# Token front of a language model tower on one Trainium2 core: first normalization and projections by halves, loads in another order

## The chip, the core and the metric

The kernel runs on one NeuronCore of a Trainium2 chip. Its engines work side by side, each through a list of instructions of its own in order, and wait for each other by semaphores: TensorE (PE, matmuls, with its weight loads shown as PEld), VectorE (DVE), ScalarE (ACT), GpSimd (POOL) and SyncE (SP, which here only issues DMAs). Matmul results stand in PSUM (`ps`, eight banks of 512 columns), all else in SBUF with 128 partitions. The metric is the device time of one execution in microseconds, the median of several runs.

## The reference, cut to what matters

Two sequences of 1024 tokens, 64 channels. The change touches the first two lines and the network `_rpe` inside the third block.

```python
h = W[x] + pe                                             # embedding + position table
h = h + linear_attn(layernorm(h), Wq, Wkv, Wproj, bproj)  # block 1
h = h + ffn(layernorm(h), ...)      # block 2: causal attention with rotary tables, 8 experts, top 2
h = h + tno(layernorm(h), ...)      # block 3: Toeplitz mixing by FFT, gate, branch
h = h + layernorm(h) @ weight.T + bias

# block 1, eight heads of eight channels
q = elu(q) + 1; k = elu(k) + 1
context = k^T v ; out = (q context) / max(q . sum(k), 1e-6) @ Wproj.T + bproj

# in block 3: the lag network, 3 layers over the lags alone, no token in it
h = idx @ pos_w.T + pos_b
for i in range(3): h = relu(srms(h)) @ rpe_lw[i].T + rpe_lb[i]
a = relu(srms(h)) @ out_w.T + out_b
```

`srms` divides by the root of the mean square over 8 channels. The kernel computes elu(x) + 1 as max(x, 0) + exp(min(x, 0)).

## The kernel before

The tokens stand in eight tiles of 128 tokens, each with both sequences' 64 channels side by side. Half 0 is tiles 0 to 3 and half 1 tiles 4 to 7, 512 columns each. The order on every engine is written out by hand: `build` has one block per engine, which it runs from top to bottom.

- **SP** (L341 to L413) issues the loads in this order: indices, `rp` (lag network), `idt` (identity), `pe_s` (positions, on `ld_pe`), the whole weight pack `w` (on `ld_w`), the rotary tables `rope_s` and `rope_k`, `bfc_s` (bf16 constants, among them the warmers' operands), two small ones. Then it waits for all gathers and issues the Fourier table `tm` and the expert weights.
- **POOL** (L416) issues sixteen gathers of embedding rows (L428), one for each tile and sequence, counted in three semaphores by `SLICES = ((0, 4), (4, 6), (6, 8))`. Later it adds the bias to `h` (L440), once both halves are normalized, and clears `va2`.
- **DVE** (L1507) runs the lag network first: `rpe_layer(0..2)` and its end `rpe_layer(3)` (L1592 to L1613), which holds the reciprocal of L1611. Then `embed(a)` for the three slices (L1615: add positions, row sums, subtract the mean), `first_sums(a)` (row sums of the squares), one variance for all (L1641), one reciprocal, and `scale_rows` for both halves (L1644, line L1567 in the profile). Then `xT` of half 1 is copied from PSUM, the transposed lag network is folded into `geo` (L1647 to L1655), and the features follow in pairs: k minima, key sums, q minima, query sums (L1659 to L1680). `cbd` is the block context, masked (L1683, L1684).
- **ACT** (L1197) takes the square roots of the lag network (L1242), the squares of the slices (`first_squares`, L1234), one root (L1247), the copy of `xT` for half 0, loads the table for Exp, and does the exponentials and the copies of v (`va1`). `next_function` (L1224) is a table load with a dummy operation.
- **PE** (L629) runs the lag network's matmuls, its two transposes (L665, L666), `keep_warm(14, 6)` (fourteen matmuls whose result nobody reads), `transposes` of both halves (L636), then k for both halves, v for both, q for both (L673 to L682), the context (L684) and the products with `cbd` (L692). `mm` is the helper at L336, whose line nearly all matmuls show.

A float32 matmul of this kernel shows as two instructions in the trace, each with a weight load of its own.

## Time and profile before

| | |
|---|---|
| median of 3 runs | 327.52 us (327.43 to 327.71) |
| profiled execution, its time | 327.58 us |
| its span (first to last instruction) | 325.8 us |
| PE busy | 291.7 us (90%) |
| DVE busy | 232.7 us (71%) |
| ACT busy | 148.2 us (45%) |
| POOL busy | 118.6 us (36%) |
| mean granted TensorE clock | 0.991 |

The busy shares are means over a long program. The change is in the first 40 us, so the tables that count are the timelines of that stretch, which show for each engine when an instruction or a run of like instructions began, how long it took, and for whom the engine had waited. A time in them is counted from the span's start.

### The profile page before, as it was taken

Reading aid. Unit: us, or ns where it says so; the run is one execution under the profiler, and the core shown is the slowest. Engines: PE = TensorE matmul, PEld = TensorE weight load, DVE = VectorE, ACT = ScalarE, POOL = GpSimd, SP = SyncE. Lnnn points to the kernel's source line nnn. Section 1 sums busy time; section 2 is a strip of 40 time slices with the busy share of each in tenths; the row PEclk is TensorE's granted clock in tenths of the full one; section 3 lists DMA queues with packets and bytes.
Section 4 is the critical chain, followed back from the end, with each engine's and each line's share of the span. In section 5 each row is a group of like instructions: output and inputs, shape, how many; then the busy total and the mean of one; then the engine's idle time right before and its main releaser. Section 6 shows DMA issues by size and latency. Waiting matters only on the chain.

```text
span 325.8 us, 4437 instructions
## 1 busy us (share of the span) xinstructions
PE 291.7 (90%) x1564; PEld 165.8 (51%) x1575; DVE 232.7 (71%) x428; ACT 148.2 (45%) x249; POOL 118.6 (36%) x168
## 2 busy tenths in 40 slices
PE   1548989999999999999999999999999999999863
PEld 1214754753332434576654555554655555557552
DVE  1577888889989778568955686744678576675576
ACT  2113634752576777846638454544533110022283
POOL 5773000331428244303323460431004689920212
PEclk9999999999999999999999999999999999999996
DMA  7957500285000000600000000000000000000001
GB/s 237 347 114 292 231 0 0 36 152 106 2 3 2 2 3 4 257 0 2 1 0 2 1 0 2 0 0 2 1 0 0 2 0 0 3 0 0 0 3 64
DMA packets 6270, 15.24 MB, mean 47 GB/s; under 512 B 1384, under 2 KB 3816, under 8 KB 5608
## 3 DMA queue, kind: packets, MB, share of 16 engines
q1 hardware_dynamic: 5685, 14.41, 14.5%
q0 software_dynamic: 512, 0.53, 0.7%
q8 instruction: 13, 0.21, 0.3%
q14 instruction: 9, 0.07, 0.1%
q10 hardware_dynamic: 51, 0.01, 0.0%
HBM read 12.01 MB, written 0.52 MB: 38 GB/s over the span
## 4 chain that ended last, share of the span: by engine, by line
PE 63%; DVE 16%; POOL 8%; issue 5%; ACT 5%; DMA 1%; another core or an unknown queue 0%; DVEq 0%; ACTq 0%
PE ps L336 60%; POOL xc L428 5%; DVE rw L1766 2%; DVE arena L1900 1%; PE ps L842 1%; DVE h L2027 1%; DMA xc<-emb,idx_s 1%; POOL share L605 1%; PE ps L636 1%; ACT L1224 1%; PE ps L1117 1%; DVE xs L1827 1%; POOL share L606 1%; ACT arena L1403 1%; DMA idx_s<-idx 0%
## 5 line engine op out<-in xcount | busy, mean ns | idle before, releaser
L1766 DVE TENSOR_REDUCE rw<-ps 128x1 f32<-128x512 f32 (+2 forms) x80 | 45.8, 629 | 7.1 <-PE ps L336 6.8
L1343 ACT ACTIVATE arena<-ps 128x1024 f32<-128x1024 f32 (+3 forms) x48 | 37.5, 812 | 21.8 <-PE ps L336 21.4
L336 PE MATMUL ps<-arena 96*128 96x512 bf16 (+7 forms) x192 | 43.2, 327 | 0.4 <-DVE rw L1766 0.2
L336 PE MATMUL ps<-xs,e_hi 128*128 128x512 f32 x96 | 40.5, 422 | 1.5 <-ACT arena L1403 0.8
L1403 ACT ACTIVATE arena<-ps 128x512 f32<-128x512 f32 x48 | 28.5, 597 | 28.1 <-PE ps L336 23.8
L1900 DVE TENSOR_TENSOR arena<-ps,arena 128x512 f32<-128x512 f32 x48 | 32.5, 687 | 11.3 <-ACT arena L1403 9.8
L336 PE MATMUL ps<-xs,e_lo 128*128 128x512 f32 x96 | 37.9, 395 | 0.0
L336 PE MATMUL ps<-bfc_s 128*128 128x512 bf16 (+2 forms) x108 | 28.4, 334 | 1.7 <-DVE xc L1623 1.5
L336 PEld LDWEIGHTS ps<-arena 96*128 96x128 bf16 (+1 forms) x192 | 15.9, 97 | 25.6 <-DVE rw L1766 11.8
L336 PE MATMUL ps<-arena,ew 64*64 64x512 f32 (+1 forms) x128 | 24.2, 609 | 1.7 <-issue 1.4
L336 PEld LDWEIGHTS ps<-xs,e_hi 128*128 128x128 f32 x96 | 18.0, 188 | 14.4 <-issue 7.2
L510 POOL TENSOR_SCALAR_AFFINE_SELECT arena<-arena 128x256 f32<-128x256 f32 (+1 forms) x32 | 15.1, 475 | 28.1 <-ACT arena L1343 27.7
L336 PE MATMUL ps<-arena,tables 128*128 128x384 f32 x64 | 21.9, 488 | 0.3 <-DVE share L2040 0.3
L336 PE MATMUL ps<-share,tables 128*128 128x384 f32 x64 | 21.8, 489 | 0.0
L336 PE MATMUL ps<-arena,va 128*32 128x512 f32 (+3 forms) x192 | 21.6, 506 | 0.2 <-POOL arena L510 0.2
L1581 DVE TENSOR_TENSOR arena<-ps,arena 128x512 f32<-128x512 f32 x16 | 10.4, 687 | 14.9 <-PE ps L336 7.5
L336 PE MATMUL ps<-w,xT 128*128 128x128 f32 (+2 forms) x144 | 19.7, 321 | 1.4 <-ACT xT L1387 1.1
L336 PEld LDWEIGHTS ps<-xs,e_lo 128*128 128x128 f32 x96 | 18.1, 189 | 2.6
L336 PEld LDWEIGHTS ps<-w,xT 128*128 128x128 f32 (+1 forms) x144 | 14.3, 188 | 9.1 <-issue 6.1
L428 POOL DMA_INDIRECT xc<-emb,idx_s x16 | 16.3, 1020 | 6.7 <-issue 4.6
L1394 ACT ACTIVATE arena<-ps 128x384 f32<-128x384 f32 x16 | 7.8, 490 | 23.4 <-PE ps L336 23.4
L1224 ACT ACT_TABLE_LOAD x14 | 18.0, 1283 | 1.0 <-PEq L2292 0.8
(273 smaller groups left out, 511.3 us busy)
## 6 DMA issues: line engine op xcount, KB each, us to landing
arena<-arena SPq DMA_DIRECT2D x24, 96.0 KB, 2.8
w<-wpack SPq DMA_DIRECT2D x1, 2089.5 KB, 10.8
arena<-tm SPq DMA_DIRECT2D x2, 1024.0 KB, 5.8
tables<-epack SPq DMA_DIRECT2D x1, 1540.0 KB, 11.0
arena<-rope SPq DMA_DIRECT2D x1, 1024.0 KB, 13.4
tables<-tu SPq DMA_DIRECT2D x2, 512.0 KB, 3.7
tables<-tk SPq DMA_DIRECT2D x2, 512.0 KB, 5.6
rp<-rpack SPq DMA_DIRECT2D x1, 678.5 KB, 4.1
```

The lines of the kernel that those rows point to most:

```text
L336: return nc.tensor.matmul(o, l, r, start=start, stop=stop, **kw)
L428: nc.gpsimd.indirect_dma_start(xc[:, j, b, :], None, emb, bass.IndirectOffsetOnAxis(ap=idx_s[:, n:n + 1], axis=0)).then_inc(gathered[[lo < ...
L510: nc.gpsimd.affine_select(out=v, in_=v, pattern=[[0, 2], [1, P + behind]], compare_op=ALU.is_ge, fill=0.0, base=-behind, channel_multiplie ...
L605: nc.gpsimd.tensor_tensor(dst[:, 0], p1[:, 0], p1[:, 1], ALU.subtract).then_inc(S("part"), 1)
L606: nc.gpsimd.tensor_tensor(dst[:, 1], p2[:, 0], p2[:, 1], ALU.add).then_inc(S("part"), 1)
L1224: nc.scalar.activation(unused[:, loads[0]:loads[0] + 1], idt[0:1, 0:1], func)
L1343: nc.scalar.activation(pt[:, n % PT_SLOTS, :, lo:512], ps[:, bank:bank + 2, lo:512], ACT.Exp, scale=HD ** -0.5).then_inc(S("exp_done"), 1)
L1394: nc.scalar.activation(dst.rearrange("p (b c) -> p b c", b=B), ps[:, UV_BANKS[k]:UV_BANKS[k] + 2, 0:D1], ACT.Silu).then_inc(S("uv_silu"), 1)
L1403: nc.scalar.activation(sil[:, m % 2], ps[:, m % 2], ACT.Silu).then_inc(S("silu"), 1)
L1581: V.tensor_tensor(zp_[:, n % 2], ps[:, 5 + n % 2], wb[:, n % 2], ALU.mult).then_inc(S("zpair"), 1)
L1766: V.tensor_reduce(top_view(m, part)[:, at:at + len(heads), i], src, AXX, ALU.max, negate=True).then_inc(S("ring_read"), 1)
L1900: V.tensor_tensor(gh[:, n % GSLOTS, n3], ps[:, 2 + m % 3], sil[:, m % 2], ALU.mult).then_inc(S("gated"), 1)
```

## The change

**Loads.** The columns of the weight pack are put in another order, so that what block 1 needs (`q1`, `kv1`, `proj1`, `bproj`, the masks) stands first, 784 of 4179 columns. This part is loaded alone, on `ld_pe` with the positions; `bfc` comes next, then the rest of `w`. The rotary tables are issued only once slice 0 is gathered.

**Order by halves.** The lag network's end is no longer one piece: its square stands behind `embed(0)`, and its root, reciprocal and last product behind the scale of half 0. Each half has a root and a scale of its own (`first_root`, `first_scale`, with the epsilon now as ACT's bias). PE projects half 0 (`first_projections(0)`: T1, k, v, q) ahead of the lag network's transposes and ten warmers, and half 1 behind them. ACT takes over both `xT` copies and the k and q minima of half 0, as Relu(-x), with exp(-x) of the result later. On DVE the first key sum stands ahead of the k minimum of half 1. POOL's bias add waits for `geo_done` as well.

```diff
-for _n, _w in (("q1", P), ("kv1", 2 * P), ("proj1", P), ("q2", P), ("q2r", P), ("k2", 64), ("k2r", 64), ("v2", 64),
+for _n, _w in (("q1", P), ("kv1", 2 * P), ("proj1", P), ("bproj", P), ("mask_c", P), ("mask_k", 16),
+               ("q2", P), ("q2r", P), ("k2", 64), ("k2r", 64), ("v2", 64),
                ("wo2", P), ("v3", 2 * D1), ("u3", 2 * D1), ("o3", 3 * P), ("t3", P), ("w4", P),
-               ("bproj", P), ("ub", 2 * D1), ("vb", 2 * D1), ("ob", 1), ("tb", P), ("b4", P), ("ln2", 1),
-               ("ln1", 1), ("cen", P), ("mask_c", P), ("mask_k", 16), ("eidx", P), ("enum", P)):
+               ("ub", 2 * D1), ("vb", 2 * D1), ("ob", 1), ("tb", P), ("b4", P), ("ln2", 1),
+               ("ln1", 1), ("cen", P), ("eidx", P), ("enum", P)):
     WCOLS[_n] = (_at, _at + _w)
     _at += _w
 WTOT = _at
+WFRONT = WCOLS["mask_k"][1]
...
-            sp.dma_start(w[:], wpack).then_inc(ld_w, 16)
-            sp.dma_start(rope_s[:], rope).then_inc(ld_rope, 16)
-            for c in range(2):
-                sp.dma_start(rope_k[64 * c:64 * c + 64], rope[0:64, :, c * 512:(c + 1) * 512]).then_inc(ld_rope, 16)
+            sp.dma_start(w[:, 0:WFRONT], wpack[:, 0:WFRONT]).then_inc(ld_pe, 16)
             sp.dma_start(bfc_s[:], bfc).then_inc(ld_bf, 16)
+            sp.dma_start(w[:, WFRONT:WTOT], wpack[:, WFRONT:WTOT]).then_inc(ld_w, 16)
             at = 3 * P + B * NPAIR * P
             for b in range(B):
                 sp.dma_start(kst[MROW:KROWS, b * NKV:b * NKV + NKV].rearrange("p g t -> p (g t)").rearrange("p (n t) -> p n t", t=P),
                              spread(bfc[0:65:32, at:at + P], 1, NKV * N // P)).then_inc(ld_ones, 16)
             for a, (lo, hi) in enumerate(SLICES):
                 sp.wait_ge(gathered[a], 16 * B * (hi - lo))
+                if a == 0:
+                    sp.dma_start(rope_s[:], rope).then_inc(ld_rope, 16)
+                    for c in range(2):
+                        sp.dma_start(rope_k[64 * c:64 * c + 64], rope[0:64, :, c * 512:(c + 1) * 512]).then_inc(ld_rope, 16)
...
             pool.wait_ge(S("n1"), 2)
-            pool.wait_ge(ld_w, 16)
+            pool.wait_ge(S("geo_done"), 2 * NW)
+            pool.wait_ge(ld_pe, 32)
...
+            def first_projections(a):
+
+                pe.wait_ge(S("n1"), a + 1)
+                for j in range(4 * a, 4 * a + 4):
+                    ins = nc.tensor.transpose(ps[:, 2 + a, j % 4 * P:(j % 4 + 1) * P], sq[:, j].rearrange("p b c -> p (b c)"), idt[:])
+                ins.then_inc(S("T1"), 1)
+                pe.wait_ge(ld_pe, 32)
+                pe.wait_ge(S(("xT1_lo", "xT1_hi")[a]), 1)
+                for x in range(2):
+                    for j in range(4 * a, 4 * a + 4):
+                        ins = mm(ps[:, 2 * x + a, j % 4 * P:(j % 4 + 1) * P], xT[:, j * P:(j + 1) * P], W("kv1", x * P, (x + 1) * P))
+                    ins.then_inc(S("kv1"), 1)
+                mm(ps[:, 4 + a], W("q1"), xT[:, a * 512:(a + 1) * 512]).then_inc(S("q1"), 1)
+
+            first_projections(0)
             pe.wait_ge(S("r_act"), LAYERS + 1)
             nc.tensor.transpose(ps[:, 7, 0:P], rh[:, 3, 0:P], idt[:])
             nc.tensor.transpose(ps[:, 7, P:2 * P], rh[:, 3, P:2 * P], idt[:]).then_inc(S("r_T"), 1)
             pe.wait_ge(ld_bf, 16)
-            pe.wait_ge(S("first_centred"), 1)
-            keep_warm(14, 6)
-
-            transposes(sq, 2, S("n1"), S("T1"))
-            pe.wait_ge(ld_w, 16)
-            for x in range(2):
-                for j in range(NT):
-                    if x == 0 and j % 4 == 0:
-                        pe.wait_ge(S(("xT1_lo", "xT1_hi")[j // 4]), 1)
-                    ins = mm(ps[:, 2 * x + j // 4, (j % 4) * P:(j % 4 + 1) * P], xT[:, j * P:(j + 1) * P],
-                             W("kv1", x * P, (x + 1) * P))
-                    if j % 4 == 3:
-                        ins.then_inc(S("kv1"), 1)
-            for c in range(2):
-                mm(ps[:, 4 + c], W("q1"), xT[:, c * 512:(c + 1) * 512]).then_inc(S("q1"), 1)
+            pe.wait_ge(S("first_centred"), 3)
+            keep_warm(10, 6)
+            first_projections(1)
...
+            def first_root(a):
+
+                act.wait_ge(S("mean_squares"), NORMS["var1"] + a)
+                nc.scalar.activation(st[:, 3, 8 * a:8 * a + 8], st[:, 1, 8 * a:8 * a + 8], ACT.Sqrt, scale=1.0 / C,
+                                     bias=eps1[:]).then_inc(S("roots"), 1)
+
+            def first_columns(a):
+
+                act.wait_ge(S("T1"), a + 1)
+                nc.scalar.copy(xT[:, 512 * a:512 * a + 512], ps[:, 2 + a]).then_inc(S(("xT1_lo", "xT1_hi")[a]), 1)
+
+            def first_values(a):
+
+                act.wait_ge(S("kv1"), 2 * a + 2)
+                nc.scalar.copy(va1[:, 4 * a:4 * a + 4, 0:P], ps[:, 2 + a].rearrange("p (j x) -> p j x", j=4)).then_inc(S("va1"), 1)
+
+            for i in range(LAYERS):
+                lag_root(i)
+            first_squares(0)
+            lag_root(LAYERS)
+            act.wait_ge(S("geo_constants"), 1)
+            first_root(0)
+            first_columns(0)
+            first_squares(1)
+            act.wait_ge(S("kv1"), 1)
+            nc.scalar.activation(kf1[:, 0:4].rearrange("p j b c -> p (j b c)"), ps[:, 0], ACT.Relu, scale=-1.0).then_inc(S("kmin"), 1)
+            first_values(0)
+            act.wait_ge(S("q1"), 1)
+            nc.scalar.activation(qf1[:, 0:512], ps[:, 4], ACT.Relu, scale=-1.0).then_inc(S("qmin"), 1)
+            first_squares(2)
+            first_root(1)
             next_function(ACT.Exp)
-            for a in range(2):
-                act.wait_ge(S("kmin"), a + 1)
-                nc.scalar.activation(kf1[:, 4 * a:4 * a + 4], kf1[:, 4 * a:4 * a + 4], ACT.Exp).then_inc(S("kexp"), 1)
-            for a in range(2):
-                act.wait_ge(S("kv1"), a + 3)
-                nc.scalar.copy(va1[:, 4 * a:4 * a + 4, 0:P], ps[:, 2 + a].rearrange("p (j x) -> p j x", j=4)).then_inc(S("va1"), 1)
-            for c in range(2):
-                act.wait_ge(S("qmin"), c + 1)
-                nc.scalar.activation(qf1[:, c * 512:(c + 1) * 512], tmp[:, c * 512:(c + 1) * 512], ACT.Exp).then_inc(S("qexp"), 1)
+            first_columns(1)
+            act.wait_ge(S("kmin"), 1)
+            nc.scalar.activation(kf1[:, 0:4], kf1[:, 0:4], ACT.Exp, scale=-1.0).then_inc(S("kexp"), 1)
+            act.wait_ge(S("qmin"), 1)
+            nc.scalar.activation(qf1[:, 0:512], qf1[:, 0:512], ACT.Exp, scale=-1.0).then_inc(S("qexp"), 1)
+            act.wait_ge(S("kmin"), 2)
+            nc.scalar.activation(kf1[:, 4:8], kf1[:, 4:8], ACT.Exp).then_inc(S("kexp"), 1)
+            first_values(1)
+            act.wait_ge(S("qmin"), 2)
+            nc.scalar.activation(qf1[:, 512:N], tmp[:, 512:N], ACT.Exp).then_inc(S("qexp"), 1)
...
+            def first_scale(a):
+
+                dve.wait_ge(S("roots"), NORMS["std1"] + a)
+                step(V.reciprocal(hst(4, a), hst(3, a)))
+                V.tensor_tensor(half3(sq, a), half3(xc, a), spread(hst(4, a), 2, C), ALU.mult).then_inc(S("n1"), 1)
+
+            def first_total(a):
+
+                lo, hi = SLICES[a]
+                dve.wait_ge(S("first_squared"), a + 1)
+                V.tensor_reduce(st[:, 1, B * lo:B * hi], sq[:, lo:hi].rearrange("p j b c -> p (j b) c"), AXX,
+                                ALU.add).then_inc(S("mean_squares"), 1)
+
+            for i in range(LAYERS):
                 rpe_layer(i)
-            dve.wait_ge(ld_pe, 16)
+            dve.wait_ge(ld_pe, 32)
             embed(0)
+            V.tensor_tensor(rh[:, 1], rh[:, 0], rh[:, 0], ALU.mult).then_inc(S("r_sq"), 1)
+            first_total(0)
+            first_scale(0)
+            dve.wait_ge(S("r_rms"), LAYERS + 1)
+            V.scalar_tensor_tensor(out=scale_r, in0=scale_r, scalar=1e-8, in1=rh[:, 2], op0=ALU.mult, op1=ALU.add).then_inc(S("r_scale"), 1)
+            dve.wait_ge(S("r_scale"), LAYERS + 1)
+            step(V.reciprocal(scale_r, scale_r))
+            V.scalar_tensor_tensor(out=rh[:, 3], in0=rh[:, 0], scalar=0.0, in1=scale_r, op0=ALU.max, op1=ALU.mult).then_inc(S("r_act"), 1)
             embed(1)
-            first_sums(0)
+            first_sums(1)
             embed(2)
-            first_sums(1)
-            first_sums(2)
-            V.tensor_scalar(st[:, 2], st[:, 1], 1.0 / C, 1e-5, ALU.mult, ALU.add).then_inc(S("mean_squares"), 1)
-            dve.wait_ge(S("roots"), NORMS["std1"])
-            step(V.reciprocal(st[:, 4], st[:, 3]))
-            scale_rows(sq, xc, 4, S("n1"))
-            evac(3, S("T1"), 2, S("xT1_hi"))
             dve.wait_ge(S("r_T"), 1)
             step(V.tensor_copy(rh[:, 1], ps[:, 7, 0:2 * P]))
+            first_total(2)
+            first_scale(1)
             others = rh[:, 1, 64:NW * 64].rearrange("p (d x) -> p d x", d=NW - 1)
             step(V.tensor_tensor(others, others, spread(rh[:, 1, 0:64], 1, NW - 1), ALU.subtract))
             dve.wait_ge(S("geo_constants"), 2)
@@ -1653,22 +1710,22 @@
                                for sd in range(2))
                 V.tensor_tensor(geo[:, 0, :, d * GR:d * GR + R], plus, minus, ALU.add).then_inc(S("geo_done"), 1)
                 V.tensor_tensor(geo[:, 1, :, d * GR:d * GR + R], plus, minus, ALU.subtract).then_inc(S("geo_done"), 1)
-            dve.wait_ge(S("xT1_lo"), 1)
-            dve.wait_ge(S("xT1_hi"), 1)
 
             k2 = kf1.rearrange("p j b c -> p (j b c)")
-            for a in range(2):
-                g = slice(512 * a, 512 * a + 512)
-                dve.wait_ge(S("kv1"), a + 1)
-                V.tensor_scalar(k2[:, g], ps[:, a], 0.0, None, ALU.min).then_inc(S("kmin"), 1)
-            for a in range(2):
+
+            def key_features(a):
+
                 g = slice(512 * a, 512 * a + 512)
                 dve.wait_ge(S("kexp"), a + 1)
                 V.scalar_tensor_tensor(out=k2[:, g], in0=ps[:, a], scalar=0.0, in1=k2[:, g], op0=ALU.max,
                                        op1=ALU.add).then_inc(S("kf1"), 1)
-            for c in range(2):
-                dve.wait_ge(S("q1"), c + 1)
-                V.tensor_scalar(tmp[:, c * 512:(c + 1) * 512], ps[:, 4 + c], 0.0, None, ALU.min).then_inc(S("qmin"), 1)
+
+            key_features(0)
+            dve.wait_ge(S("kv1"), 3)
+            V.tensor_scalar(k2[:, 512:N], ps[:, 1], 0.0, None, ALU.min).then_inc(S("kmin"), 1)
+            dve.wait_ge(S("q1"), 2)
+            V.tensor_scalar(tmp[:, 512:N], ps[:, 5], 0.0, None, ALU.min).then_inc(S("qmin"), 1)
+            key_features(1)
```

On DVE, from the last full lag layer to the first slice's square sums and on to the second slice, there stood:

```order
L1608 SCALAR_TENSOR_TENSOR share<-tmp,rp,ps 128x256 [waits r_lin,r_scale]
L1596 TENSOR_TENSOR share<-share 128x256 [waits dve_chain]
L1603 SCALAR_TENSOR_TENSOR tmp<-tmp,share 128x256 [waits r_rms]
L1611 RECIPROCAL tmp<-tmp 128x256 [waits r_scale]
L1612 SCALAR_TENSOR_TENSOR share<-share,tmp 128x256 [waits dve_chain]
L1621 TENSOR_TENSOR h<-xc,share 128x512 [waits gathered_0,ld_pe]
L1622 TENSOR_REDUCE st<-h 128x8 [waits dve_chain]
L1623 SCALAR_TENSOR_TENSOR xc<-st,h 128x512 [waits dve_chain]
L1621 TENSOR_TENSOR h<-xc,share 128x256 [waits gathered_1]
L1622 TENSOR_REDUCE st<-h 128x4 [waits dve_chain]
L1623 SCALAR_TENSOR_TENSOR xc<-st,h 128x256 [waits dve_chain]
L1630 TENSOR_REDUCE st<-sq 128x8 [waits first_squared]
```

and there stands (L1694 to L1697 are the lag network's end, L1676 and L1677 the scale of half 0):

```order
L1649 SCALAR_TENSOR_TENSOR share<-tmp,rp,ps 128x256 [waits r_lin,r_scale]
L1662 TENSOR_TENSOR h<-xc,share 128x512 [waits gathered_0,ld_pe,dve_chain]
L1663 TENSOR_REDUCE st<-h 128x8 [waits dve_chain]
L1664 SCALAR_TENSOR_TENSOR xc<-st,h 128x512 [waits dve_chain]
L1690 TENSOR_TENSOR share<-share 128x256
L1683 TENSOR_REDUCE st<-sq 128x8 [waits first_squared]
L1676 RECIPROCAL st<-st 128x8 [waits roots]
L1677 TENSOR_TENSOR sq<-xc,st 128x512 [waits dve_chain]
L1694 SCALAR_TENSOR_TENSOR tmp<-tmp,share 128x256 [waits r_rms]
L1696 RECIPROCAL tmp<-tmp 128x256 [waits r_scale]
L1697 SCALAR_TENSOR_TENSOR share<-share,tmp 128x256 [waits dve_chain]
L1662 TENSOR_TENSOR h<-xc,share 128x256 [waits gathered_1]
```

The embedding, the sums and the scale of half 0 have moved ahead of the reciprocal of the lag network; the second slice comes behind it.

On ACT, from the lag network's last roots to the table load for Exp, there stood:

```order
L1242 ACTIVATE share<-ps 128x256 [waits r_ss]
L1242 ACTIVATE share<-ps 128x256 [waits r_scale,r_ss] x3
L1234 ACTIVATE sq<-xc 128x512 [waits first_centred]
L1234 ACTIVATE sq<-xc 128x256 [waits first_centred] x2
L1247 ACTIVATE st<-st 128x16 [waits mean_squares]
L1210 COPY xT<-ps 128x512 [waits T1]
L1224 ACT_TABLE_LOAD
L1224 ACTIVATE unused<-idt 1x1
```

and there stands (L1254 is the lag root, L1281 the k minimum of half 0, L1284 its q minimum, L1245 the squares):

```order
L1245 ACTIVATE sq<-xc 128x512 [waits first_centred]
L1254 ACTIVATE share<-ps 128x256 [waits r_scale,r_ss]
L1259 ACTIVATE st<-st,eps 128x8 [waits mean_squares,geo_constants]
L1265 COPY xT<-ps 128x512 [waits T1]
L1245 ACTIVATE sq<-xc 128x256 [waits first_centred]
L1281 ACTIVATE share<-ps 128x512 [waits kv1]
L1270 COPY share<-ps 128x4x128 [waits kv1]
L1284 ACTIVATE share<-ps 128x512 [waits q1]
L1245 ACTIVATE sq<-xc 128x256 [waits first_centred]
L1259 ACTIVATE st<-st,eps 128x8 [waits mean_squares]
L1235 ACT_TABLE_LOAD
```

The squares of the third slice now stand behind three instructions that read half 0's projections from PSUM.

On PE, behind the lag network's last matmul, there stood:

```order
L336 MATMUL ps<-share,rp 128x256 [waits r_sq]
L665 MATMUL ps<-idt,share 128x128 [waits r_act]
L666 MATMUL ps<-idt,share 128x128
L336 MATMUL ps<-bfc_s 128x512 [waits first_centred,ld_bf]
L336 MATMUL ps<-bfc_s 128x512 x13
L636 MATMUL ps<-idt,sq 128x128 [waits n1]
L636 MATMUL ps<-idt,sq 128x128 x3
L636 MATMUL ps<-idt,sq 128x128 [waits n1]
L636 MATMUL ps<-idt,sq 128x128 x3
L336 MATMUL ps<-w,xT 128x128 [waits xT1_lo,ld_w]
L336 MATMUL ps<-w,xT 128x128 x3
```

and there stands (L675 are the transposes of a half, L687 and L688 those of the lag network):

```order
L339 MATMUL ps<-share,rp 128x256 [waits r_sq]
L675 MATMUL ps<-idt,sq 128x128 [waits n1]
L675 MATMUL ps<-idt,sq 128x128 x3
L339 MATMUL ps<-w,xT 128x128 [waits xT1_lo,ld_pe]
L339 MATMUL ps<-w,xT 128x128 x7
L339 MATMUL ps<-xT,w 128x512
L687 MATMUL ps<-idt,share 128x128 [waits r_act]
L688 MATMUL ps<-idt,share 128x128
L339 MATMUL ps<-bfc_s 128x512 [waits first_centred,ld_bf]
L339 MATMUL ps<-bfc_s 128x512 x9
L675 MATMUL ps<-idt,sq 128x128 [waits n1]
```

The transposes, the eight k and v matmuls and the q matmul of half 0 have moved ahead of the lag network's transposes and the warmers.

## Rows read from the trace of the kernel before

**Rows 1.** The page, chain that ended last: shares of the span by engine
```profile
PE 63%; DVE 16%; POOL 8%; issue 5%; ACT 5%; DMA 1%; another core or an unknown queue 0%; DVEq 0%; ACTq 0%
```

**Rows 2.** Timeline, DVE and ACT: start us, us, engine, line, operation, [idle before]
```profile
15.35 0.48 DVE L1608 SCALAR_TENSOR_TENSOR share<-tmp,rp,ps 128x256 f32<-128x256 f32 x1
...
18.48 1.75 DVE L1611 RECIPROCAL tmp<-tmp 128x256 f32<-128x256 f32 x1
...
20.61 0.68 DVE L1621 TENSOR_TENSOR h<-xc,share 128x512 f32<-128x512 f32 x1
...
22.78 0.63 ACT L1234 ACTIVATE sq<-xc 128x512 f32<-128x512 f32 x1 [4.79 <-DVE xc L1623]
...
25.25 0.43 DVE L1621 TENSOR_TENSOR h<-xc,share 128x256 f32<-128x256 f32 x1 [0.66 <-DMA xc<-emb,idx_s]
...
26.63 0.42 ACT L1234 ACTIVATE sq<-xc 128x256 f32<-128x256 f32 x1 [2.18 <-DVE xc L1623]
...
27.81 0.22 ACT L1247 ACTIVATE st<-st 128x16 f32<-128x16 f32 x1 [0.76 <-DVE st L1641]
28.06 0.25 DVE L1643 RECIPROCAL st<-st 128x16 f32<-128x16 f32 x1 [0.28 <-ACT st L1247]
28.34 1.29 DVE L1567 TENSOR_TENSOR sq<-xc,st 128x512 f32<-128x512 f32 x2
```

**Rows 3.** Landing of the eighth gather, of the last two gathers, and of `w`
```profile
DMA to landing us min/median/max: 7.5/7.5/7.5
...
DMA to landing us min/median/max: 2.7/2.8/2.8
...
w<-wpack SPq DMA_DIRECT2D x1, 2089.5 KB, 10.8
```

**Rows 4.** Timeline, PE and PEld: last lag matmuls, the warmers, their last weight loads
```profile
16.35 1.22 PE L336 MATMUL ps<-share,rp 128*128 128x256 f32 x2 [1.10 <-DVE share L1596]
...
22.89 4.83 PE L336 MATMUL ps<-bfc_s 128*128 128x512 bf16 x14 [1.45 <-DVE xc L1623]
...
26.26 0.97 PEld L336 LDWEIGHTS ps<-bfc_s 128*128 128x128 bf16 x5 [0.28 <-issue]
```

**Rows 5.** Timeline of PE at the kernel's end; busy time by stretch (clock: last but two)
```profile
312.87 1.06 PE L336 MATMUL ps<-w4c,xT 128*128 128x128 f32 x8
...
319.72 2.02 PE L336 MATMUL ps<-w4c,xT 128*128 128x128 f32 x8 [0.79 <-ACT xT L1483]
...
320.00:321.00 1.00, 1.00 (x6) 1.00 (x6) 0.97 (x3) 0.60 (x1) 0.14 (x1) 0.50 0.00 0
```

**Rows 6.** Timeline, all engines, from the transposes to the products with `cbd`
```profile
29.72 2.36 POOL L440 TENSOR_TENSOR h<-h,w 128x1024 f32<-128x1024 f32 x1 [5.19 <-DVE sq L1567]
29.79 0.59 ACT L1210 COPY xT<-ps 128x512 f32<-128x512 f32 x1 [1.76 <-PE ps L636]
...
30.39 1.28 ACT L1224 ACT_TABLE_LOAD   x1
...
30.52 3.81 PE L336 MATMUL ps<-w,xT 128*128 128x128 f32 x32 [0.17 <-ACT xT L1210]
...
31.44 0.79 DVE L1649 TENSOR_TENSOR share<-share 128x128 f32<-128x128 f32 x1
...
34.16 1.88 PE L336 MATMUL ps<-xT,w 128*128 128x512 f32 x4
...
36.85 1.31 DVE L1677 SCALAR_TENSOR_TENSOR share<-ps,share 128x512 f32<-128x512 f32 x2
...
38.08 0.28 DVE L1683 TENSOR_TENSOR cbd<-ps,w 128x128 f32<-128x128 f32 x1
...
38.56 2.23 PE L336 MATMUL ps<-cbd,share 128*128 128x144 f32 x16 [0.73 <-DVE cbd L1684]
```

**Rows 7.** Timeline, DVE and POOL side by side in the expert stage
```profile
150.16 0.68 DVE L1900 TENSOR_TENSOR arena<-ps,arena 128x512 f32<-128x512 f32 x1
...
150.32 0.32 POOL L547 TENSOR_TENSOR rw<-rw 128x64 f32<-128x64 f32 x1 [1.11 <-DVE rw L1861]
```

More of the change, by code:

```diff
@@ L45 @@
                                              "wpc_zero"))}
-NORMS = {"var1": 1, "var2": 2, "var2b": 4, "var3": 5, "var3b": 6, "var4": 7,
-         "std1": 1, "std2": 2, "rms2b": 4, "std3": 5, "rms3b": 6, "std4": 7}
+NORMS = {"var1": 1, "var2": 3, "var2b": 5, "var3": 5, "var3b": 6, "var4": 7,
+         "std1": 1, "std2": 3, "rms2b": 5, "std3": 5, "rms3b": 6, "std4": 7}
 EARLY_AF = 3
@@ L297, in build @@
         unused = sb("unused", [1, 16])
+        eps1 = sb("eps1", [P, 1])
         w4c = sb("w4c", [P, P])
@@ L566, in _ @@
             candidates(1, 1)
-            pool.wait_ge(S("mean_squares"), 5)
+            pool.wait_ge(S("mean_squares"), 6)
             PT(st[:, 3, 0:8], st[:, 2, 0:8], halves[:], ALU.pow).then_inc(S("roots"), 1)
@@ L1237, in _, with lag_root @@
             nc.scalar.activation(rh[:, 0], RP("lag"), ACT.Identity, scale=RP("pw"), bias=RP("pb")).then_inc(S("r_h"), 1)
-            for i in range(LAYERS + 1):
+            def lag_root(i):
                 act.wait_ge(S("r_ss"), i + 1)
@@ L1242, in _ @@
                 nc.scalar.activation(rh[:, 2], ps[:, 0, 0:2 * P], ACT.Sqrt, scale=1.0 / R).then_inc(S("r_rms"), 1)
-            for a in range(len(SLICES)):
-                first_squares(a)
-            act.wait_ge(S("mean_squares"), NORMS["var1"])
-            nc.scalar.activation(st[:, 3], st[:, 2], ACT.Sqrt).then_inc(S("roots"), 1)
-            evac(2, S("T1"), 1, S("xT1_lo"))
-            next_function(ACT.Exp)
-            for a in range(2):
-                act.wait_ge(S("kmin"), a + 1)
-                nc.scalar.activation(kf1[:, 4 * a:4 * a + 4], kf1[:, 4 * a:4 * a + 4], ACT.Exp).then_inc(S("kexp"), 1)
@@ L1292, in _ @@
                     second_roots(1)
+            act.wait_ge(ld_w, 16)
             evac(2, S("T2"), 1, S("xT2_lo"), scale=W("ln1"))
@@ L1584, in _ @@
             dve.wait_ge(ld_rp, 16)
+            V.memset(eps1[:], 1e-5)
             V.memset(geo[:], 0.0).then_inc(S("geo_constants"), 1)
@@ L1681, in _ @@
             dve.wait_ge(S("ctx1"), 1)
+            dve.wait_ge(ld_pe, 32)
             dve.wait_ge(ld_w, 16)
@@ L1816, in second_scale @@
                 if b == 0:
-                    dve.wait_ge(S("roots"), 5 - a)
+                    dve.wait_ge(S("roots"), 6 - a)
                     step(V.reciprocal(hst(4, a), hst(3, a)))
@@ L1919, in third_scale @@
             def third_scale(a):
-                dve.wait_ge(S("roots"), 7 - a)
+                dve.wait_ge(S("roots"), 8 - a)
                 step(V.reciprocal(hst(4, a), hst(3, a)))
```

8 lines of the change are left out of this document (4 added, 4 removed).

## The prediction

> **What bounds the kernel now.** I read the chain of waits first. PE holds 63% of it and POOL 8% [rows 1]; the POOL part is the front, where sixteen gathers go out one after another, and the change touches only this front. So the question is when the front hands over. I take as the handover the matmuls of the query features with the block context (`cbd`): they start at 38.56 us [rows 6], everything behind them is unchanged and starts one thing after another, and so a shift there should reach the end.
>
> Then I read the timelines of DVE and ACT. The lag network's last full layer ends at 15.83 (15.35 + 0.48); its end goes on until 20.6, with a reciprocal of 1.75. Half 0 (slice 0) is embedded from 20.61. The last slice is embedded at 25.25, after a wait of 0.66 for the last gather. Both halves then wait for one common root and are scaled from 28.34 to 29.63 [rows 2]. From there DVE has the longest list: the second xT copy, the lag features, two key minima, two key sums, two query minima, two query sums, `cbd`. The row of one list entry shows a stall: L1649, 128 columns in 0.79, running until 32.23 while POOL's bias add runs from 29.72 to 32.08 [rows 6].
>
> **The change, part by part.** I take times in the profiled run: span 325.8, its own time 327.58, so 1.78 lie around the span. The median of the three runs is 327.52.
>
> *Half 0 early.* `embed(0)` now follows the last full lag layer: 15.87, if slice 0 is there. In the trace of before the eighth gather, the last of slice 0, was issued at 11.75 and took 7.5 to land (19.25), but the last ones took 2.7 to 2.8 [rows 3]; between them lies the end of the big loads. Of these, `w` (2089.5 KB) landed 10.8 after its issue at 2.64, at 13.4. In the new order the same bytes up to `w`, and 384 KB of `bfc`, are ahead of the gathers' end, and `rope` with `rope_k` (1536 KB) goes out only behind slice 0. So I put the landing at the low end: the eighth gather at 14.5 (11.75 + 2.7) to 15.5 (the backlog behind 13.4 plus about a microsecond for `bfc`). The bounds are 14.5 and 19.25.
>
> Then, each step from its row [rows 2]: embedding 0.68 + 0.69 + 0.69 with gaps, to 18.0; the square on ACT 0.63 beside the lag's own square on DVE; PE's sum for the lag and its latency 1.26 (its two matmuls take 1.22 [rows 4]), so ACT takes the last lag root at 19.8 (0.38, my estimate from the same 256 columns as the squares of 0.42). It stands ahead of the new `first_root(0)` on ACT. Root 0.22, reciprocal 0.25, scale 0.69: half 0 is scaled at about 21.4. Transposes, xT copy: at the pace of before 0.76 + 0.59, 21.5 to 22.9.
>
> *The rate of PE decides the next term.* In the trace of before the lag network's matmuls of 256 columns, and the first warmers of 512, run at half their later pace: fourteen warmers begin at 22.89 and take 4.83; their last five weight loads need 0.97 from 26.26, about 0.2 each, and the nine before that, of which the first two go together, make eight steps in 3.37, 0.42 each [rows 4]. By the spacing this is 1.2 GHz and then 2.4 GHz (the granted clock reads 1.00 in this stretch, so I go by the spacing). The end of the kernel gives the price directly: the same eight w4 matmuls of 128 columns take 1.06 at clock 1.00 and 2.02 at clock 0.50 [rows 5]. Before the new half-0 projections PE has only had bursts of the lag network (the last is 1.22 long, at 16.35, now at 18.5) with idle time between. I take it as at the lower rate: transposes about 1.25 for 0.66, so k starts at 23.5. k, v and q of one half cost 3.81/4 + 3.81/4 + 1.88/2 = 2.84 at the high rate [rows 6] and 5.7 to 5.9 at the low one. If the rate rises as late behind the start of the back-to-back stretch as it did there (22.89 to 26.26), it does so at 26.9 and q ends at 28.05; if it rises at 27.7 (my middle), at 28.45; if not before the end, at 29.4; at the high rate throughout, at 26.4.
>
> The Trainium skill says in "TensorE: Matmul & The Clock Gate", section Part 4: PE-mode transpose, that transposes do not count as PE work in the same way for the clock. No row here separates them; by that page the four transposes of half 0 would not bring the rise forward, which speaks against the gain, and the sum would keep its middle or its late end.
>
> *What is queued behind that.* On ACT the order is now: squares of slice 1, k minimum of half 0, v copy, q minimum of half 0, and only then the squares of slice 2 and `first_root(1)`. So half 1's normalization waits for half 0's q on PE. From q's end: 0.08 + 0.60 (Relu, as the copy's 0.59), squares 0.42, sum 0.42, root 0.22, reciprocal 0.2, scale 0.69, latencies about 0.2: 2.85. The other input of this point is DVE: after 21.4 it still has the lag's end (0.42 + 1.75 + 0.42), slice 1's embedding 1.34, its squares and sum 0.95, then slice 2's embedding 1.35, to 27.8 where before had it at 26.6. So the last gather no longer waits for anyone; DVE does. Scaling of half 1 therefore ends at 30.0 at the earliest (before: 29.63), and at 31.3 with my middle.
>
> *Half 1 afterwards.* From the end of its scale, T: 0.76 to the copy's start, 0.59 copy (now ACT; the Exp table load of 1.28 + 0.2 goes just ahead of it, from T - 0.95 to T + 0.55, hidden by 0.2), 0.13, then k, v, q 2.84: T + 4.35. Behind q on DVE: q minimum, second key sum, two query sums at 0.65 each, then 0.48 of `cbd`: T + 7.55. The context matmuls of half 1 (about 0.95) are hidden under the two query sums (1.31). Before, this took 38.56 - 29.63 = 8.93. So the second part is cheaper by 1.4: one copy, one key minimum and sum, one q minimum have left DVE's list, and L1649's stall too, since POOL's add now waits for `geo_done`.
>
> That added wait of POOL has its add, 2.36 long, and two memsets behind it; the add then ends near T + 3.3, and the reader at L1691 comes after 38.56, so it costs nothing. It now lies beside a DVE sum with one input in PSUM, at T + 2.05. The row for that is L1900, with a POOL add beside it: 0.68, not stretched [rows 7]. If it were held until POOL's end, the DVE list would move by 0.2; I take nothing. The Trainium skill ("GPSIMD Engine Reference", Specifications) says the shared SBUF interface is contended only by DVE instructions with two SBUF inputs or in a 2-port mode. L1649 has two SBUF inputs and ends 0.15 behind POOL, so the trace agrees; by that page the cost here is nothing, and by plain overlap it would be the 0.2.
>
> *The warmers.* Ten instead of fourteen, behind the r_T transposes: from 28.45 + 0.5, 2.13 at the high rate, to 31.1; T1 of half 1 is ready at 31.35. Covered by a quarter of a microsecond, and uncovered (up to 0.4) only if the rate rises very late. *Loads:* `rope`, now issued near 15, is first read by the rotary products, far behind the handover. The rest of `w` comes at about 13 and is first read there too. The changed semaphore numbers and the `eps1` memset (under 0.1, before 6.25, where DVE waited) cost nothing.
>
> **The sum.** T = 28.45 + 2.85 = 31.3; handover 31.3 + 7.55 = 38.85; before 38.56. Shift +0.3: 327.9 against this run, 327.8 against the median. This is the time of "nearly nothing": 1.4 gained in the second part, 1.7 lost because half 1 is scaled later.
>
> **Rivals.**
> (a) *PE is fast early, faster.* If the rate has risen by 25.7 or is high from the start, q of half 0 is out by 26.4 to 27.4, the ACT queue no longer matters, and DVE's list sets T at 30.0: handover 37.5, -1.1, 326.4. For it: every later stretch is at the high rate. Against it: four bursts and the warmers in the same region were slow [rows 4]. It is below 0.2% from a rise before 25.7.
> (b) *PE stays slow, slower.* The mechanism is the q minimum of half 0 ahead of slice 2's squares on ACT. With a rise later than 28.4, q ends at 28.8 to 29.4, T = 31.7 to 32.3, handover 39.2 to 39.8: +0.7 to +1.25, 328.2 to 328.8, about 328.5. It decides from 28.4 on. [...]
> (c) *The loads don't clear the way.* If slice 0 lands as in the trace of before, at 19.25, the whole front moves by 3.4, less the idle time of ACT and PE it absorbs: +2.4 to +3.3, near 330.4. Below a landing of 15.9 nothing is lost, then nearly 1 for 1 in DVE's list. Against it: the last gathers' 2.7.
> (d) *It doesn't do what it says*, the last gather still setting the end: that would need DVE free at 25.25, and its own list keeps it until 26.4. I give it no chance apart from (a).
>
> **How the numbers follow.** Forecast (rise between 25.7 and 28.4, shift -0.65 to +0.65): 0.42. (a) 0.24. (b) 0.28. (c) 0.06. The faster case is (a), 0.24; slower is (b) and (c), 0.34; the bound is 0.2% or 0.65 us, about what a measurement can tell from no change. The range takes (a) down to 326.2 and (b) up to 329.0, and leaves (c) out.
>
> **What would show it.** In the profile after: `embed(0)` at 15.9 (gather); spacing of the half-0 k and v matmuls near 0.24 (slow) or 0.12 (fast), and where it changes; ACT's squares of slice 2 right behind the q minimum rather than behind DVE's centring at 27.8; half 1 scaled at 31.3; L1649's counterpart near 0.2 instead of 0.79; the `cbd` matmuls at 38.85. I am wrong if half 0's projections run at the high rate from the start, if slice 0 is late, or if a shift at the handover is given back behind it, where I count none.

## Result and profile after

The changed kernel took 328.26 us (median of 20 runs, 327.52 to 328.67) against 327.70 for the kernel before (20 runs, 327.05 to 328.01): 1.0016, 95% interval 1.0010 to 1.0022. That is 0.5 us slower; the ratio lies inside the forecast's bound of 0.2% for no change, the upper end of its interval a little outside. In the ratios here and below, two long executions with a lower granted clock are left out, one of the kernel before (332.86 us) and one of the kernel before with POOL's wait (491.61 us). The profiled run of the changed kernel took 327.75 (span 326.0), that of before 327.58 (span 325.8); so the traces can explain 0.2 us of the 0.5. The profiled run is one of the faster of its 20.

The first group is from the page, chain that ended last: POOL's share has fallen from 8% [rows 1] to 3%, and PE's has risen from 63% to 69%.

```profile
PE 69%; DVE 15%; ACT 6%; issue 4%; POOL 3%; DMA 1%; another core or an unknown queue 0%; SPq 0%; DVEq 0%; ACTq 0%
```

Timeline of the kernel after, half 0 (start us, us, engine, line, operation, idle before and what ended it); the last line but one is gather 12's wait:

```profile
15.90 0.69 DVE L1662 TENSOR_TENSOR h<-xc,share 128x512 f32<-128x512 f32 x1
...
20.52 0.69 DVE L1677 TENSOR_TENSOR sq<-xc,st 128x512 f32<-128x512 f32 x1
...
23.15 3.75 PE L339 MATMUL ps<-w,xT 128*128 128x128 f32 x16 [0.77 <-ACT xT L1265]
...
24.20 0.43 DVE L1662 TENSOR_TENSOR h<-xc,share 128x256 f32<-128x256 f32 x1 [0.41 <-DMA xc<-emb,idx_s]
...
26.70 1.49 PE L339 MATMUL ps<-xT,w 128*128 128x512 f32 x2
```

Half 0 is embedded at 15.90 and scaled at 21.21 (20.52 + 0.69). The same sixteen k and v instructions (eight matmuls, two instructions each) take 3.75 for half 0 and 2.02 for half 1 (below); q takes 1.49 against 1.02. So PE ran at its lower rate and came to the higher one within q. The granted clock that the profile gives for this stretch reads 1.00 all the same, and the rate is read from the durations; in the last experiment the same sixteen take 3.75 in a stretch whose granted clock reads 0.50.

Timeline of the kernel after, half 1:

```profile
27.39 0.42 DVE L1664 SCALAR_TENSOR_TENSOR xc<-st,h 128x256 f32<-128x256 f32 x1
...
28.22 0.60 ACT L1284 ACTIVATE share<-ps 128x512 f32<-128x512 f32 x1 [0.69 <-PE ps L339]
28.24 2.32 PE L339 MATMUL ps<-bfc_s 128*128 128x512 bf16 x10
...
28.71 0.41 ACT L1245 ACTIVATE sq<-xc 128x256 f32<-128x256 f32 x1
...
30.25 0.69 DVE L1677 TENSOR_TENSOR sq<-xc,st 128x512 f32<-128x512 f32 x1
30.86 0.28 DVE L1706 TENSOR_TENSOR share<-share 128x128 f32<-128x128 f32 x1
31.00 0.42 PEld L675 LDWEIGHTS ps<-idt,sq 128*128 128x128 f32 x4 [0.93 <-DVE sq L1677]
...
32.02 2.36 POOL L446 TENSOR_TENSOR h<-h,w 128x1024 f32<-128x1024 f32 x1 [7.77 <-issue]
...
32.42 2.02 PE L339 MATMUL ps<-w,xT 128*128 128x128 f32 x16 [0.77 <-ACT xT L1265]
...
35.34 0.69 DVE L1727 TENSOR_SCALAR tmp<-ps 128x512 f32<-128x512 f32 x1 [1.06 <-PE ps L339]
...
38.38 2.23 PE L339 MATMUL ps<-cbd,share 128*128 128x144 f32 x16 [0.53 <-DVE cbd L1742]
...
40.17 0.55 DVE L1750 RECIPROCAL rw<-rw 128x64 f32<-128x64 f32 x1 [0.22 <-DVE rw L1749]
```

Slice 2 is centred at 27.81, but its squares start at 28.71, since ACT first does half 0's q minimum (L1284), which waits for PE. Half 1 is scaled at 30.94; in the kernel before it was at 29.63 [rows 2]. The products with `cbd` start at 38.38, 0.18 ahead of before [rows 6]. Then the reciprocal of the denominators has 0.22 of idle time in front, where before had none, and the two kernels are level again by 40.17 (before: 40.18). Further on the offset grows slowly, to 0.04 near 71 us, 0.10 near 220 and 0.17 at the end, with nothing in the trace that names a cause. That much may be the tail of a single execution: in the experiments below, two kernels hand over at 36.75 and 36.76, the first with the 0.22 in front of its reciprocal and the second without, and their spans are 324.3 and 324.4. So it is not shown that the 0.22 reaches the end.

### The profile page after: what moved, and what is told of

It is laid out like the page before. It is cut to its first block, busy times and chain, and to the rows that moved or that the text cites. A ratio compares the mean times of both kernels' runs of the same rounds, so it can differ in the third digit from the quotient of the medians.

```text
span 326.0 us, 4434 instructions
## 1 busy us (share of the span) xinstructions
PE 291.1 (89%) x1560; PEld 166.4 (51%) x1571; DVE 230.6 (71%) x426; ACT 149.9 (46%) x253; POOL 118.2 (36%) x168
## 4 chain that ended last, share of the span: by engine, by line
PE 69%; DVE 15%; ACT 6%; issue 4%; POOL 3%; DMA 1%; another core or an unknown queue 0%; SPq 0%; DVEq 0%; ACTq 0%
PE ps L339 65%; DVE rw L1824 2%; DVE arena L1958 1%; PE ps L853 1%; DMA idt<-ident 1%; DVE h L2085 1%; POOL share L611 1%; ACT L1235 1%; PE ps L1128 1%; ACT arena L1443 1%; DVE xs L1885 1%; POOL share L612 1%; PE ps L675 1%; DVE share L1649 0%; POOL rw L502 0%
## 5 line engine op out<-in xcount | busy, mean ns | idle before, releaser
L339 PE MATMUL ps<-bfc_s 128*128 128x512 bf16 (+2 forms) x104 | 25.9, 314 | 0.2
L339 PE MATMUL ps<-w,xT 128*128 128x128 f32 (+2 forms) x144 | 21.6, 339 | 2.8 <-ACT xT L1265 1.5
L339 PEld LDWEIGHTS ps<-w,xT 128*128 128x128 f32 (+1 forms) x144 | 16.0, 204 | 10.9 <-issue 7.8
```

What stands on the lines that cost most here:

```text
L339: return nc.tensor.matmul(o, l, r, start=start, stop=stop, **kw)
```

## Experiments

Every ratio is to the kernel before, run on the same chip in the same session (median 327.58 to 327.69 us). T is the end of the half-1 scale, "handover" the start of the products with `cbd`.

**PE at its higher rate early.** Eleven matmuls on the warmers' operands are added, seven ahead of the last lag sum and four ahead of half 0's transposes.

```diff
+                if i == LAYERS:
+                    pe.wait_ge(ld_bf, 16)
+                    keep_warm(7, 6)
...
+            keep_warm(4, 6)
             first_projections(0)
```

> The changed kernel with eleven more warmers: seven ahead of the lag network's last sum, four ahead of the transposes of half 0. Nothing else moves. Theory A (PE projects half 0 at its lower rate, and the q minimum of half 0 holds the squares of slice 2 on ACT): q of half 0 ends near 25.6 instead of 28.1, the squares of slice 2 start right behind DVE's centring at 27.9, half 1 is scaled at 30.0 instead of 30.9, the cbd matmuls start near 37.5, and the median falls by 1 to 1.5 us, to 0.996 to 0.998 of the kernel before. Theory B (DVE's own list sets the front): no change beyond 0.2 us, 1.0015. Theory C (the gain is given back behind the handover, as 0.18 us was in the profiled run): handover near 37.5, but the span falls by less than half of the 0.9 us.

Measured: 326.54 us, ratio 0.9967 (0.9954 to 0.9980). Timeline of this kernel:

```profile
22.46 2.02 PE L339 MATMUL ps<-w,xT 128*128 128x128 f32 x16 [0.77 <-ACT xT L1269]
23.93 0.42 DVE L1666 TENSOR_TENSOR h<-xc,share 128x256 f32<-128x256 f32 x1 [0.36 <-DMA xc<-emb,idx_s]
24.32 1.02 PE L339 MATMUL ps<-xT,w 128*128 128x512 f32 x2
...
27.57 0.42 ACT L1249 ACTIVATE sq<-xc 128x256 f32<-128x256 f32 x1 [0.40 <-DVE xc L1668]
...
29.11 0.69 DVE L1681 TENSOR_TENSOR sq<-xc,st 128x512 f32<-128x512 f32 x1
```

k and v of half 0 take 2.02 and q is out at 25.34, so the squares of slice 2 now follow DVE's centring and not the q minimum. T is 29.80 and the handover 37.24. The price of the low rate is thus 1.14 us at T, and as much at the handover; of this 0.9 reaches the end of the profiled run (span 325.1 for 326.0). The median gained more, 1.6 us by the two ratios, so the low rate may account for a part of the 0.5 us that the kernel after lost; no trace of a slower execution of it shows that. This kernel beats both.

**The squares of slice 2 ahead of half 0's q minimum** on ACT, and the lag copy behind the half-1 scale on DVE.

```diff
+            first_squares(2)
             act.wait_ge(S("q1"), 1)
             nc.scalar.activation(qf1[:, 0:512], ps[:, 4], ACT.Relu, scale=-1.0).then_inc(S("qmin"), 1)
-            first_squares(2)
             first_root(1)
```

> The changed kernel with slice 2's squares ahead of the q minimum of half 0 on ACT, and the lag copy behind half 1's scale on DVE. The rate of PE in half 0's projections stays as it is. Theory A: the squares start at 27.9 instead of 28.7, half 1 is scaled near 30.2 instead of 30.9, PE's warmers then end last (near 30.5), T1 of half 1 starts there, 0.4 to 0.5 us earlier than in the change; the median falls by about 0.5 us, to 1.000 of the kernel before, and by more in executions with a late rise of the rate. Theory B (PE's own row of instructions, not ACT's queue, is what counts): T1 of half 1 stays at 31.0 and the time at 1.0016.

Measured: 327.36 us, ratio 0.9989 (0.9978 to 0.9999). Timeline of this kernel:

```profile
26.72 1.91 PE L339 MATMUL ps<-xT,w 128*128 128x512 f32 x2
...
27.45 0.42 ACT L1245 ACTIVATE sq<-xc 128x256 f32<-128x256 f32 x1
...
28.85 2.52 PE L339 MATMUL ps<-bfc_s 128*128 128x512 bf16 x10
...
29.72 0.69 DVE L1677 TENSOR_TENSOR sq<-xc,st 128x512 f32<-128x512 f32 x1
...
31.21 0.60 PE L675 MATMUL ps<-idt,sq 128*128 128x128 f32 x4
```

The squares start 1.26 earlier and T comes at 30.41, 0.53 earlier. In this execution PE stayed at the low rate through q (1.91), which ended 0.44 later than in the kernel after; counted from q's end, T comes 0.97 earlier. It is not free of q even so, since half 1's root still stands behind the q minimum on ACT (29.16, with the sum done at 28.32). The warmers ran until about 31.2, and it is they that half 1's transposes now follow, 0.8 behind T; the handover is at 38.53, no earlier than in the kernel after. The median is by its ratio 0.9 us below that of the kernel after; its twelve executions spread from 326.63 to 328.01 and the traced one is among the slower, so others may keep the gain, which no trace shows. So the place of slice 2's squares behind the q minimum costs at least 0.5 at T, the mechanism of rival (b), and behind it stand the warmers, which are late for the same reason.

**The old place of the rotary tables.** `rope` and `rope_k` go out ahead of `bfc` and the gathers' end, as in the kernel before, and so does the rest of `w`; its front part stays a load of its own.

```diff
+            sp.dma_start(w[:, WFRONT:WTOT], wpack[:, WFRONT:WTOT]).then_inc(ld_w, 16)
+            sp.dma_start(rope_s[:], rope).then_inc(ld_rope, 16)
+            for c in range(2):
+                sp.dma_start(rope_k[64 * c:64 * c + 64], rope[0:64, :, c * 512:(c + 1) * 512]).then_inc(ld_rope, 16)
             sp.dma_start(bfc_s[:], bfc).then_inc(ld_bf, 16)
-            sp.dma_start(w[:, WFRONT:WTOT], wpack[:, WFRONT:WTOT]).then_inc(ld_w, 16)
...
-                if a == 0:
-                    sp.dma_start(rope_s[:], rope).then_inc(ld_rope, 16)
...
```

> The changed kernel with rope and rope_k back ahead of bfc and of the gathers' end, the split of w kept. Theory A (the loads part is what lets slice 0 land in time): slice 0 lands near 19.2 instead of 15.2, embed(0) starts there, the handover moves by 2.4 to 3.3 us, median near 331, 1.008 to 1.010. Rival (the gathers land early whatever is queued): embed(0) stays at 15.9, time 1.0016.

Measured: 331.98 us, ratio 1.0126 (1.0109 to 1.0142). Timeline of this kernel:

```profile
19.87 0.69 DVE L1661 TENSOR_TENSOR h<-xc,share 128x512 f32<-128x512 f32 x1 [3.71 <-DMA xc<-emb,idx_s]
...
30.67 1.90 PE L339 MATMUL ps<-xT,w 128*128 128x512 f32 x2
...
42.76 1.49 PE L339 MATMUL ps<-cbd,share 128*128 128x144 f32 x10 [0.53 <-DVE cbd L1741]
```

Slice 0 is late by 3.97 and the handover by 4.38: nothing on the way absorbs it. The 0.41 on top are PE's rate: half 0's q took 1.90 for 1.49 and so ended 4.38 later. The reordering of the loads is the part on which the change stands.

**Both: PE early, rotary tables behind the last loads of the front.**

```diff
-                if a == 0:
-                    sp.dma_start(rope_s[:], rope).then_inc(ld_rope, 16)
...
+            sp.dma_start(rope_s[:], rope).then_inc(ld_rope, 16)
...
```

> As early_warm, with rope and rope_k issued behind tm, so nothing large is on the DMA queues while the last gathers land. With PE out of the way DVE's list is the bound (theory A'): slice 1 is embedded at 23.8 instead of 24.2, everything behind it 0.4 us earlier than in early_warm, 0.001 lower. If instead the landing of slice 2 sets the front, embed(2) does not move.

Measured: 326.07 us, ratio 0.9963 (0.9949 to 0.9977). Timeline of this kernel:

```profile
23.44 0.42 DVE L1665 TENSOR_TENSOR h<-xc,share 128x256 f32<-128x256 f32 x1
...
28.62 0.69 DVE L1680 TENSOR_TENSOR sq<-xc,st 128x512 f32<-128x512 f32 x1
```

Slice 1 no longer waits for its gather, T is 29.31 and the handover 36.75, both 0.49 earlier than with PE early alone.

**The rotary tables late, alone.** The same edit on the kernel after.

> The kernel after with rope and rope_k issued behind the last of the front's loads, so that the last gathers don't run beside them. Theory A (the squares of slice 2 stand behind half 0's q minimum on ACT, and PE's rate sets that): gather 12's wait of 0.43 us on DVE goes, slice 2 is centred at 27.4 in place of 27.8, and the half-1 scaling still ends at 30.9: ratio to the kernel before 1.001 to 1.002. Rival (DVE's list sets the half-1 scaling): everything is 0.4 us earlier and the ratio is 1.000 to 1.0005.

Measured: 327.88 us, ratio 1.0007 (0.9998 to 1.0015), its interval overlapping that of the kernel after, and between what the two theories have; the trace decides. Timeline of this kernel:

```profile
27.01 0.43 DVE L1663 SCALAR_TENSOR_TENSOR xc<-st,h 128x256 f32<-128x256 f32 x1
...
28.28 0.60 ACT L1283 ACTIVATE share<-ps 128x512 f32<-128x512 f32 x1 [0.64 <-PE ps L339]
...
28.77 0.41 ACT L1244 ACTIVATE sq<-xc 128x256 f32<-128x256 f32 x1
```

Slice 2 is centred 0.37 earlier (27.44) and its squares start at 28.77, no earlier; the handover is at 38.43. DVE's list does not set T in the kernel after; PE's rate does, through ACT's queue. With PE fast, the same edit moved T by 0.49.

**POOL's wait for the lag products, in the kernel before.**

```diff
+            pool.wait_ge(S("geo_done"), 2 * NW)
```

> The kernel before with one part of the change alone: POOL's bias add waits for the six lag products on DVE. Theory A (the sharing of the bus is what stretched L1649 to 0.79 us): the row falls to about 0.3 us, DVE's list and the cbd matmuls move by 0.5 us ahead of 38.56, to about 38.1, ratio 0.9985. Rival (the list of DVE is not what sets the handover): the row falls, but cbd stays at 38.5 and the ratio is 1.000. Second rival: POOL's add, now late by about 2 us, is itself waited for; then the ratio is over 1.001.

Measured: 327.79 us, ratio 0.9998 (0.9989 to 1.0007), as the first rival has it. Timeline of this kernel:

```profile
31.43 0.29 DVE L1650 TENSOR_TENSOR share<-share 128x128 f32<-128x128 f32 x1
...
32.60 2.37 POOL L441 TENSOR_TENSOR h<-h,w 128x1024 f32<-128x1024 f32 x1 [7.99 <-issue]
...
35.21 0.69 DVE L1672 TENSOR_SCALAR tmp<-ps 128x512 f32<-128x512 f32 x1 [0.16 <-PE ps L336]
...
36.07 0.69 DVE L1672 TENSOR_SCALAR tmp<-ps 128x512 f32<-128x512 f32 x1 [0.17 <-PE ps L336]
```

The row falls from 0.79 to 0.29. Of the half microsecond 0.33 turns into the two waits for PE's q; the products with `cbd` start at 38.54, 0.02 earlier. The stall [rows 6] was real, but PE's q stood next to it: a shorter list on DVE alone brings nothing.

**The kernel after without that wait.**

```diff
-            pool.wait_ge(S("geo_done"), 2 * NW)
```

> The kernel after without POOL's wait for the lag products. Its add would then run from about 30.0 to 32.4 us, over the scaling of half 1 and the lag products at 30.9 to 32.0. Theory A (two SBUF inputs on DVE are held by POOL's add): the products end only with the add, 0.4 to 0.6 us later than in the kernel after, but DVE then waits for PE's keys anyway (it idled 0.96 us ahead of the key sum at 32.84), so at most 0.2 us reaches the cbd matmuls and the ratio to the kernel before is 1.001 to 1.002, as with the wait. Rival (no cover): the handover moves from 38.38 to 38.9 and the ratio is 1.003 or more.

Measured: 328.00 us, ratio 1.0016 (1.0005 to 1.0028). Timeline of this kernel:

```profile
31.06 2.35 POOL L445 TENSOR_TENSOR h<-h,w 128x1024 f32<-128x1024 f32 x1 [6.71 <-DVE sq L1676]
31.21 2.25 DVE L1710 TENSOR_TENSOR share<-share 128x32 f32<-128x32 f32 x1
...
35.37 0.69 DVE L1726 TENSOR_SCALAR tmp<-ps 128x512 f32<-128x512 f32 x1 [0.20 <-PE ps L339]
```

A product of 32 columns, elsewhere 0.19, takes 2.25 and ends 0.05 behind POOL's add. The two key steps behind it slide by 0.9 to 1.1, and the q minimum starts where it did, its wait for PE down from 1.06 to 0.20. So the stall is 2.1, far larger than the 0.4 to 0.6 expected, and still covered. The wait for `geo_done` costs nothing and brings nothing in this order. By the 0.20 of idle time that is left, a q from PE more than 0.2 earlier would make it worth having; that is an estimate, and no run shows it.

**All edits together** (PE early, tables late, squares early, lag copy late, six warmers in place of ten), then the same kernel once more in another session, and two kernels that undo parts of it: one with ten warmers again, one with ACT's and DVE's order of the kernel after.

> The kernel after with four edits at once: matmuls ahead of half 0's transposes to have PE at its high rate there, rope behind the last loads, the squares of slice 2 ahead of half 0's q minimum on ACT and the lag copy behind the half-1 scaling on DVE, six warmers in place of ten. With the first two alone the median was 326.07 us. Theory A (once PE is at the high rate, half 0's q is out before slice 2 is centred, and ACT's order no longer decides): the same within 0.2 us, 325.9 to 326.3, less 0.4 if the lag copy leaves DVE's list ahead of the scaling, 0 if the list behind takes it up again. Rival (ACT's queue still costs): 325.5 or less.

> The kernel of all_three once more, unchanged, in another session: it was 2.4 us slower than the kernel before instead of 1.5 faster, with ACT's copy of half 0's transposes starting 3.9 us behind their last matmul. Theory A (it belongs to the program): about 330.1 us again and the same idle time of 5.6 us ahead of the copy. Rival (it belonged to that chip or session): 325.9 to 326.3 us and the copy at 21.9 us.

> all_three with ten warmers ahead of half 1 in place of six; all else as there (matmuls ahead of half 0, rope late, the squares of slice 2 early, the lag copy behind the scaling). If the number of warmers brings the late copy about, this one is at 325.9 to 326.3 us; if ACT's or DVE's order does, it is near 330 us.

> early_warm_late_rope with six warmers ahead of half 1 in place of ten; ACT's and DVE's order as in the kernel after. If the number of warmers brings the late copy about, this one is near 330 us; if ACT's or DVE's order does, it is at 326.0 to 326.3 us. Four warmers fewer are 0.85 us of matmuls that ended ahead of the scaled half 1 there.

Measured: 330.09 us the first time (6 runs, 329.75 to 330.37, ratio 1.0072), 326.08 the second (4 runs, 325.80 to 326.17, ratio 0.9954, 0.9934 to 0.9973), with ten warmers 326.02 (0.9948, 0.9928 to 0.9968), with six warmers and the ACT and DVE order of the kernel after 326.19 (0.9961, 0.9945 to 0.9978). Timelines of the first and the second session, and between them busy time by stretch in the first (the granted clock is the last figure but two):

```profile
21.17 0.66 PE L677 MATMUL ps<-idt,sq 128*128 128x128 f32 x4 [0.84 <-issue]
...
25.76 0.58 ACT L1268 COPY xT<-ps 128x512 f32<-128x512 f32 x1 [5.61 <-remote]
...
26.49 3.75 PE L339 MATMUL ps<-w,xT 128*128 128x128 f32 x16 [4.66 <-ACT xT L1268]
```

```profile
23.20:26.00 2.80, 0.00 (x0) 0.00 (x0) 1.64 (x5) 0.24 (x1) 1.06 (x6) 0.57 0.06 12
```

```profile
21.09 0.66 PE L677 MATMUL ps<-idt,sq 128*128 128x128 f32 x4 [0.84 <-DVE sq L1680]
...
21.78 0.59 ACT L1268 COPY xT<-ps 128x512 f32<-128x512 f32 x1 [1.71 <-PE ps L677]
...
28.64 0.69 DVE L1680 TENSOR_TENSOR sq<-xc,st 128x512 f32<-128x512 f32 x1
```

In the first session the profiled run's copy started 3.9 us behind the last transpose; PE then stood idle, its granted clock fell (0.57 on average from 23.20 to 26.00, 0.50 from 26 to 30), and k and v of half 0 ran at the low rate (3.75). In the second, on another chip, nothing of it. So the program alone does not bring it about, nor does its number of warmers. What held the copy stays open: the profile names only "remote" as its releaser, and it came in one session alone. For the order itself: T is 29.33, as it was with PE early and the tables late alone (29.31). Once PE is at the higher rate, ACT's order no longer counts. The four kernels with PE early and the tables late, the first session apart, took 326.02 to 326.19 us, 0.4% to 0.5% less than the kernel before; their intervals overlap, and none is shown to be the best.

## Why the prediction was right, and where only by luck

The time was 328.26 for 327.8 and inside the range. Point by point:

- **The loads clear the way: right.** The eighth gather landed 3.4 us after its issue at 11.77, at 15.2 (forecast 14.5 to 15.5; 7.5 before [rows 3]), and half 0 was embedded at 15.90 for 15.87. Rival (c) is what the old load order gives, and its price of 2.4 to 3.3 was too small: 4.4. Slice 0 came 3.97 late for 3.4, ACT and PE absorbed none of it, and half 0's q took 0.41 more.
- **Half 0 scaled at 21.4, k at 23.5:** 21.21 and 23.15.
- **PE's rate: right, and the middle of it.** Half 0's k and v ran at the low rate throughout and the rate rose within q: q ended at 28.19 for 28.45. This was the deciding term, as the experiment with early matmuls shows (T at 29.80 for 30.94). Rival (a) did not come about in this kernel, but brought about on purpose it gives 326.54 where the text has 326.4. The prediction cites the Trainium skill ("TensorE: Matmul & The Clock Gate", Part 4: PE-mode transpose), which says that transposes do not count as PE work in the same way for the clock; no run here separates them.
- **ACT's queue: right.** q's end to T was 2.75 for 2.85, T 30.94 for 31.3; DVE's list ended at 27.81 for 27.8. That last agreement is luck: the rows named in the prediction add up to 27.63 and not 27.8, half 0 was scaled 0.2 earlier than forecast, and 0.41 of the 27.81 is a wait for gather 12, where the text had looked at the last gather alone. Gather 12, issued 1.76 behind `rope`, took 7.2 to land (4.8 before). It cost nothing, because ACT was later.
- **Half 1 afterwards: size right, reason wrong.** T to handover took 7.44 for 7.55. The text puts the saving of 1.4 down to what left DVE's list and to L1649's stall. The runs show that PE's list had to become shorter too: taking the stall out of the kernel before gives 0.02, since DVE then waits for PE's q. In the kernel after half the projections are done before T, and the q minimum waits 1.06 for PE, so there it is PE's list that binds. What the shorter list on PE would have given alone no run shows.
- **The wait for `geo_done` costs nothing: right.** The key sum beside POOL's add took 0.69, not stretched. The Trainium skill ("GPSIMD Engine Reference", Specifications) has only DVE instructions with two SBUF inputs or in a 2-port mode contend. The runs agree: products with two SBUF inputs 0.79 and 2.25 beside the add and 0.28 and 0.19 away from it, the sum with one input in PSUM unchanged.
- **The warmers: right.** They ended at 30.56 for 31.1, 0.44 ahead of the transposes. With a late rise of the rate they bind, as the second experiment shows.
- **"Everything behind is unchanged": the step that failed.** The handover shift was -0.18 in place of +0.3, made of steps each a little quicker than forecast. Then 0.17 was given back at the reciprocal and another 0.18 lost until the end, where the prediction counts none. Errors of -0.48 and +0.35 us nearly cancelled: that the profiled run came out at +0.17 for +0.3 is luck. The median came out at +0.56, of which no single trace shows more than those 0.17; the rest stays open.
